# Routed rows outside the 512-row units: 35 units of 128 rows between the large units, in place of 21 units of 256

## The reference, cut to what matters

```
logits = flat @ gate_W.T ; top_v, top_i = top_k(softmax(logits), 2)      # 8 experts, 8192 tokens
g = silu(einsum('td,edf->etf', flat, w1_e)) ; u = einsum('td,edf->etf', flat, w3_e)
out_e = einsum('etf,efd->etd', g * u, w2_e)                              # f = 512
routed = einsum('te,etd->td', gates, out_e)                              # two experts a token
shared = the same form with one expert of width 512 for all tokens, divided by 8
ffn = 0.5 * shared + 0.5 * routed ; out = x + attention(xn) * silu(ffn)
```

## Time and profile before

| what | value |
|---|---|
| median of 3 runs | 722.14 us |
| the profiled execution's span | 719.3 us |
| what lies around its span, against the median | 2.8 us |
| TensorE matmuls busy | 654.1 us, 91% |
| VectorE busy | 555.4 us, 77% |
| ScalarE busy | 494.9 us, 69% |
| GpSimd busy | 478.9 us, 67% |
| mean granted TensorE clock | 0.988 |

### The profile page before, as it was taken

The page is one execution under the profiler, slowest core; times in us unless marked ns, Lnnn a source line. Parts: engine busy times, 40 slices in busy tenths (PEclk is TensorE's granted clock), DMA queues, the critical chain, the costliest instruction groups (busy, mean ns, idle before and its releaser), DMA issues.

```text
span 719.3 us, 22370 instructions
## 1 busy us (share of the span) xinstructions
PE 654.1 (91%) x8536; PEld 452.1 (63%) x8536; DVE 555.4 (77%) x1058; ACT 494.9 (69%) x1008; POOL 478.9 (67%) x519
## 2 busy tenths in 40 slices
PE   2787897978999999999999999999997899999993
PEld 1544565646665665566666666878886676777772
DVE  5989986877667886667766676667664899999996
ACT  4864798857665656666666666666665788888872
POOL 4844321244777777777777777767778487888873
PEclk9999999999999999999999999999999999999997
DMA  9931111111111323433323334333362767777762
GB/s 243 299 95 45 45 61 46 45 51 36 48 49 49 108 91 108 137 108 108 110 92 109 106 106 139 110 101 108 97 103 93 237 179 230 216 229 222 233 176 59
DMA packets 88616, 86.75 MB, mean 121 GB/s; under 512 B 11394, under 2 KB 65284, under 8 KB 88516
## 3 DMA queue, kind: packets, MB, share of 16 engines
q1 hardware_dynamic: 79428, 66.70, 29.8%
q0 software_dynamic: 9088, 18.63, 9.6%
HBM read 50.82 MB, written 34.47 MB: 119 GB/s over the span
## 4 chain that ended last, share of the span: by engine, by line
PE 53%; DVE 13%; ACT 12%; POOL 11%; issue 7%; DMA 3%; SPq 0%; POOLq 0%; DVEq 0%; ACTq 0%
PE banks L1556 7%; PE banks L1558 7%; PE banks L1557 7%; PE banks L1596 5%; DVE hidden L1218 4%; POOL expert_rows L644 4%; PE banks L1576 4%; PE banks L1577 4%; PE banks L1575 4%; POOL srows L634 3%; ACT hidden L785 3%; PE banks L1621 3%; PE banks L1693 3%; PE banks L1672 3%; ACT rows L823 2%
## 5 line engine op out<-in xcount | busy, mean ns | idle before, releaser
L785 ACT CAST hidden<-hidden 128x512 f16<-128x512 f32 x206 | 127.1, 617 | 135.5 <-DVE hidden L1218 135.4
L634 POOL DMA_INDIRECT srows<-normed_rows,source x142 | 149.7, 1054 | 60.4 <-issue 40.2
L1222 DVE TENSOR_TENSOR hidden<-hidden 128x512 f16<-128x512 f32 x180 | 124.4, 691 | 83.9 <-ACT hidden L785 83.0
L1218 DVE TENSOR_TENSOR hidden<-hidden,banks 128x512 f32<-128x512 f32 x206 | 140.8, 684 | 44.0 <-ACT hidden L781 38.2
L1575 PE MATMUL banks<-wwords,hidden 128*128 (+1 forms) x824 | 148.8, 219 | 1.5 <-DVE hidden L1222 1.1
L1576 PE MATMUL banks<-wwords,hidden 128*128 (+1 forms) x824 | 148.6, 219 | 0.0
L1577 PE MATMUL banks<-wwords,hidden 128*128 (+1 forms) x824 | 148.6, 219 | 0.0
L781 ACT ACTIVATE hidden<-banks 128x512 f32<-128x512 f32 x206 | 122.7, 596 | 28.1 <-PE banks L1558 27.8
L1556 PE MATMUL banks<-sx,wwords 128*128 128x512 f16 (+1 forms) x368 | 121.5, 330 | 3.2 <-DVE wwords L1013 2.7
L1558 PE MATMUL banks<-sx,wwords 128*128 128x512 f16 (+1 forms) x368 | 121.6, 330 | 0.0
L1557 PE MATMUL banks<-sx,wwords 128*128 128x512 f16 (+1 forms) x368 | 121.5, 330 | 0.0
(11 more groups left out here) (218 smaller groups left out, 1429.7 us busy)
## 6 DMA issues: line engine op xcount, KB each, us to landing
rows<-x SPq DMA_DIRECT2D x32, 256.0 KB, 4.9
rows<-expert_rows SPq DMA_DIRECT2D x32, 256.0 KB, 3.6
normed_rows<-rows SPq DMA_DIRECT2D x16, 256.0 KB, 3.9
r_rows<-rows SPq DMA_DIRECT2D x16, 256.0 KB, 2.1
rd_rows<-rows SPq DMA_DIRECT2D x16, 256.0 KB, 2.2
stage<-r_rows SPq DMA_DIRECT2D x16, 256.0 KB, 4.0
k_rows<-rows SPq DMA_DIRECT2D x16, 256.0 KB, 2.2
kd_rows<-rows SPq DMA_DIRECT2D x16, 256.0 KB, 2.2
```

The source lines that it names most:

```text
L634: G.indirect_dma_start(srows[:, q % NXB, t, :], None, rows_in, bass.IndirectOffsetOnAxis(source[:, at:at + 1], 0)).then_inc(sem[f"s_in{q % ...
L785: A.copy(guh[:, i % 4, :], gu[:, i % 2, :]).then_inc(sem["gu_hi"], 1)
L1218: V.tensor_tensor(gu[:, i % 2, :], sg[:, i % 2, :], psum[2 * (i % 2) + 1][:, :], ALU.mult).then_inc(sem["gated"], 1)
L1222: V.tensor_tensor(gul[:, i % 4, :], gu[:, i % 2, :], guh[:, i % 4, :], ALU.subtract).then_inc(sem["gu_lo"], 1)
```

## The change

The 21 units of 256 rows become 35 units of 128 rows ("pieces"). A piece has one step that holds all four channel blocks side by side: `columns` gives four blocks of 128 columns, so `pe_up` of a piece is 24 matmuls of 128 columns, with sixteen register instructions, and its `pe_down` twelve matmuls with eight. There are now 16 shared, 25 wide and 35 piece units: 199 steps. Two pieces stand at steps 48 and 49. The other 33 are spread between the 29 large units left, mostly one behind each, so that the pattern is wide, piece, wide, piece.

The groups of a wide unit stay 256 rows (50 of them), that of a piece is 128 rows (35), with buffers of their own (`trows`, `tx`, `ty`, two of each). `flip_step` puts the transposes of a wide unit two and one steps before its first step, and that of a piece one step before, or earlier where the next group would otherwise fall on the same step. GpSimd's order is now by step: `gather_step` is the step behind the transpose that frees the buffer, `scatter_step` a unit's last step plus five. There are 135 gathers and 135 scatters in place of 142 and 142. The `pe_part` steps begin at step 68.

```diff
+        order = [("shared", i) for i in range(FIRST)] + [("piece", i) for i in range(EARLY_PIECES)]
+        large = [("wide", i) for i in range(WIDES)]
+        for m in range(MIXED):
+            large.insert((m + 1) * (WIDES + MIXED) // (MIXED + 1), ("shared", FIRST + m))
+        placed = EARLY_PIECES
+        for n, unit in enumerate(large):
+            order.append(unit)
+            until = EARLY_PIECES + (n + 1) * (PIECES - EARLY_PIECES) // len(large)
+            order += [("piece", i) for i in range(placed, until)]
+            placed = until
...
+        steps = [(v, j) for v in range(NU)
+                 for j in range(1 if order[v][0] == "piece" else 4)]
...
+        for q in reversed(range(GROUPS_IN)):
+            v, h = groups[q]
+            due = first_step_of[v] - (1 if piece(v) else 2 - h)
+            flip_step[q] = min(due, flip_step[q + 1] - 1) if q + 1 < GROUPS_IN else due
+        for q, (v, h) in enumerate(groups):
+            p = last_in_slot(q, NXB, 2)
+            due = FIRST_STEPS - 2 if p is None else flip_step[p] + 1
+            gather_step[q] = max(due, gather_step[q - 1]) if q else due
+            scatter_step[q] = first_step_of[v] + (1 if piece(v) else 4) + LAG + 1
...
-            at = j - (2 if wide(v) else 0) if len(todo) == 1 else j // 2 if wide(v) and j % 2 == 0 else -1 if wide(v) else j
...
-        PART_STEP = 75
+        PART_STEP = 68
...
-            for q in range(ROUTED + SCATTER_LAG):
-                if q < ROUTED:
-                    pool_sorted(q)
-                if q >= SCATTER_LAG:
-                    pool_scatter(q - SCATTER_LAG)
+            for i in range(FIRST_STEPS - 2, NS + LAG + 2):
+                for q in groups_at(i, scatter_step):
+                    pool_scatter(q)
+                for q in groups_at(i, gather_step):
+                    pool_sorted(q)
...
-                return [(2 * j + c, c * UNIT, UNIT) for c in range(2)]
+                return [(c, c * P, P) for c in range(FC)]
...
-                        T.wait_ge(sem["s_lo"], blocks[-1] + 1)
+                        T.wait_ge(sem["s_lo"], mine[-1] + 1)
```

More of the change, by code:

```diff
@@ L34, with constants @@
 CONST = {}
-def constants(routed):
+def constants(ntok):
     p = np.arange(P)
@@ L159, in build @@
         sxh, sxl = [sx[:, i, :, :] for i in range(2)]
+        tx = sb("tx", [P, 2, 2, P], F16)
+        txh, txl = [tx[:, i, :, :] for i in range(2)]
         hidden = sb("hidden", [P, 8 * 2 * UNIT])
@@ L293, in build @@
         FIRST = SHARED - MIXED
[L294 to L308, removed]
+        EARLY_PIECES = 2
+        order = [("shared", i) for i in range(FIRST)] + [("piece", i) for i in range(EARLY_PIECES)]
[8 more added lines that the diff above has]
+            placed = until
         LAG = 3
-        steps = [(v, j) for v in range(NU) for j in range(2 if order[v][0] == "narrow" else 4)]
+        steps = [(v, j) for v in range(NU)
+                 for j in range(1 if order[v][0] == "piece" else 4)]
         NS = len(steps)
@@ L1529, in columns @@
                 v, j = steps[i]
-                if wide(v):
+                if not piece(v):
                     return [(j, 0, WIDE)]
-                return [(2 * j + c, c * UNIT, UNIT) for c in range(2)]
+                return [(c, c * P, P) for c in range(FC)]
             def pe_up(i):
@@ L1539, in pe_up @@
                 if routed(v):
[L1540 removed]
+                    mine = groups_of(v)
                     if v == FIRST and j == 0:
@@ L1543, in pe_up @@
                     if j == 0:
-                        T.wait_ge(sem["s_lo"], blocks[-1] + 1)
-                    q = blocks[0] % RING
-                    mh, ml = [a[:, q:q + len(blocks), :].rearrange("p b i -> p (b i)") for a in (sxh, sxl)]
+                        T.wait_ge(sem["s_lo"], mine[-1] + 1)
+                    mh, ml = pair_of(mine[0])
+                    if not piece(v):
+                        q = ring(mine[0], RING, 2)[0]
+                        mh, ml = [a[:, q:q + 2, :].rearrange("p b i -> p (b i)") for a in (sxh, sxl)]
                 else:
@@ L1738, in pe_program @@
                 if i >= LAG:
-                    load = steps[i][0] + 1 if i < NS and last_step_of(i) and routed(steps[i][0] + 1) else None
+                    load = steps[i][0] + 1 if i + 1 < NS and last_step_of(i) and routed(steps[i][0] + 1) else None
                     pe_down(i - LAG, load)
```

146 lines of the change are left out of this document (89 added, 57 removed).

## The result

The changed kernel takes 766.76 us (median, 763.39 to 767.95), beside 722.94 us for the kernel before on the same chip (four runs; 722.14 was the median of the first three): a ratio of 1.0607 [1.0577, 1.0636]. The forecast was 746.7 with a range up to 765. The sign was right and the size was not. The profiled execution took 766.12 us, with a span of 764.3, 45.0 more than the 719.3 of before.

The account below looks back on a forecast made before the run. TensorE, without gaps, was taken to bound the routed phase: 354.7 work + 29.5 transpose waits + 14.0 feed + 0.4 late gathers = 398.6 us against 374.0, so 722.1 becomes 746.7 us, range 729 to 765.

Parts of the forecast that it names:

- Part 1: Routed phase, TensorE's pure work: fewer steps bring it to 354.7 us, a gain of about 14 us.
- Part 2: Transposes one step before their use: TensorE waits for low halves at wide units and late pieces, 29.5 us (25 to 35).
- The covered ones: Six wide units with an attention part following on TensorE: wait covered but for 0.2 us each, 1.2 in all.
- The late pieces: Six pieces transposed at the step before: one covered by an attention part, five waiting 0.85 us each, 4.3 together.
- Part 3: Feeding TensorE register instructions and an expert's address load for each of 35 pieces: 0.40 us each, 14.0 (0 to 37).
- upper end: Per piece, 0.48 us for the expert's load plus 0.6 for register instructions, about 1.05; 37 us over all pieces.
- the feed-bound one: Sequencer limits every piece: 21 us more, 15 after overlap with waits, about 762 us; chance 0.17.
- Part 4: GpSimd's queue, 14 DMA instructions shorter: no longer behind, late gathers fall from 3.6 to 0.4 us.
- What would show it: Timeline signs: TensorE idle 1.1 to 1.7 us before wide units some 24 times, busy share of the phase about 92%.
- the pair in the list of waits: TensorE's `pe_up` waiting for the low half before wide units: total should go from 0.5 us to over 20.
- "0.07 to 0.09": Spacing in us of a piece's `pe_up` matmuls where the feed limits them, 0.055 otherwise.

Follow-up runs that it names:

- all three at once: Changed kernel with transposes from the fifth group on one step earlier, pieces on expert 0's weights at a fixed address, no expert loads before pieces: 711.87 us, 0.9853.
- the last mended kernel: Changed kernel with transposes a step earlier (pieces' three), experts loaded early, attention parts moved, 26 directly before pieces; everything computed: 715.53 us, 0.9907.

## Why the prediction was right or wrong

**Part 1** held: with the waits and the feed taken away the phase is 361.4, and the costs measured step by step add up to the 62.5 us between 354.7 and 417.2, with nothing left for the pure work to be off by. No other source of gain shows in all three at once and in the last mended kernel, the two that are faster than before.

**Part 2** held as a sum, 29.5 forecast and 29.5 measured, though by luck in its items. Wide units cost 1.04 each, not 1.15 to 1.5: from transpose to `pe_up` 1.85 to 2.00 us, and the lateness behind a part that I took from the earlier trace rows didn't add up, since TensorE waits in between and the others catch up; in the run without loads, where TensorE is sooner, those six units do wait 1.44 to 1.57. The covered ones cost 0.38 each, not 0.2, and for another reason: the part covers the low half in full, and the 0.38 are the gap of the load. So "the load before a wide unit falls into the stall of part 2 and costs nothing" was right at 19 units and wrong at these six, 2.1 us. The late pieces cost 7.4, not 4.3; one of them (step 135) 2.09. The old kernel with late transposes shows the mechanism of the wait by itself at five units, and the run that takes the waits away shows what they hide: the loads before wide units came up, 9.6 us, as soon as their cover was gone.

**Part 3** is the step that failed, in the value that I chose and not in the mechanism. "I take 0.40, nearer the lower end, since the row of the load is of a wholly dry queue" was wrong: 28 of 35 pieces were fed from a dry queue. Measured are 29.3 us, 0.84 a piece, against 14.0; the bounds of 0 to 37 held. In the kernel before, register instructions and loads were hidden, as said: the 461 distances between neighbouring 256-column matmuls of its narrow steps from 171 us on are 0.10 or 0.11, and of 157 `pe_down` only the one of step 51 has a gap at the load, the 0.53 of the earlier trace rows. After, I read the runs so (the trace doesn't show how far the sequencer is): the waits for low halves that stand in front of the transposes and of each wide unit keep it at TensorE's heels, and the 0.67 us of a wide step's `pe_down` are too short to win a lead. Only six pieces directly behind an attention part ran at 1.34, and one two steps behind a part at 1.41. The piece at step 105 stands directly behind a part as well and took 2.21: its own low half was late, and the wait for it stood between the part and the piece. The row of the part was at hand: where long matmuls stand before a piece and no wait between, the feed is free, and where not, the rows of the dry queue are the ones to take. With gaps of the load before 21 pieces, 21 x 0.48 + 28 x 0.6 = 27 would have been the sum. No run shows the 0.6 us of feed in the upper end, with which the 1.05, the 37 and the rival's 21 were made; the runs show 0.66 at each of the 28 pieces, and 0.04 for one register instruction where 0.10 was read from the earlier trace rows. The fixed weights (16.4 us back) and the missing loads (8.8 in the steps before pieces, 6 in the time) confirm both halves.

**The rival** that came true is the feed-bound one, in 28 of the 35 pieces. Its price was 21 over the forecast, 767.7 in full, and I took 6 off for overlap with the waits. There is no overlap, as the feed lies at pieces and the waits at wide units: 766.8 was measured. The range ended at 765, too low by 1.8. That 767.7 lies so near is in part luck: part 3 came to 29.3 and not to 35, and 3.7 came from a cost that nobody had named. By the time of a `pe_up` alone, some 2.0 us, a pace of 0.084 for each pair of weight load and 128-column matmul would have passed as well, and the runs with fixed weights, at 0.055, refute it here.

**Not in the forecast**: 3.7 us of transposes that wait because the one before them, on the step before, has not been copied out. I had looked at who waits for the low half of a group and not at the group behind it. The start of the phase came 2.3 us later, but it lies between 171.0 and 173.4 in the profiles of all these kernels, the old one's variant among them. 2.3 + 43.2 - 0.5 at the end is the 45.0 of the spans.

**Part 4** held: no late gathers, GpSimd waits for results. **What would show it**: TensorE's busy share of the phase is 93% (about 92% said), and the idle before wide units is there 19 times (24 said). But the pair in the list of waits went to 10.8 us and not over 20. At 358.71 the stretch is 1.03 us too long, and only 0.48 of it stand in that line: 0.36 are the load's gap at 357.73, put down to issue or lost in recorded lengths, and 0.165 the recorded length of the last matmul beyond its pace. I had priced by distances and then named a view that counts otherwise. And "0.07 to 0.09" between matmuls of a fed piece was right in the mean (0.25 for three), while each three has two at 0.055 and one at 0.13.

## What to carry to other kernels

Before tiles are made smaller, count what each one needs beside its work (register instructions, loads of an index, waits), and ask of each place whether long work stands directly before it; if the queue is dry there, take the dry queue's price in full (here 0.66 us for the `pe_up` of a piece, and mostly 0.4 to 0.6 for a load). Keep two steps between a producer chain of three engines and its consumer (one step in place of two cost the old kernel 22 us), and check the producer of the group behind it as well. A wait that comes true just before TensorE gets there costs more than its own length: loads and register instructions behind it lose their cover, in the old kernel too (10.4 us of loads behind 9.1 of such waits). A cost that lies inside a wait is not gone: removing the wait alone gave back 20 of 30 us, and only all edits together the whole.

## What the runs showed of the hardware

With a dry queue two register instructions lengthen three 128-column matmuls from 0.165 to 0.25 us, 0.04 each (step 115: 2.01 us with sixteen of them, 1.34 without), in line with one triple after another of the piece at 355.26:
```profile
L1617 PE MATMUL banks<-tx,wwords 128*128 128x128 f16 x280 | 59.0, 226 | 7.4 <-DVE tx L1272 5.9
```
The group's idle time of 7.4 us (part 5 of the page after) holds nothing of it: all of this cost is hidden in matmuls recorded as 0.22 us long. The load of an expert's number into a register leaves mostly 0.4 to 0.6 us between two matmuls of TensorE with a dry queue (0.59 at 353.85, 0.42 at 202.71; 0.10 to 0.67 at 45 places of the kernel after, 41 of them from 0.35 up), and none at step 89 (0.06 from 286.32 to 286.38), whose piece stands behind six 512-column matmuls. With no register instructions in the 24 of a piece's `pe_up`, 36 pairs of weight load and 128-column matmul ran at 0.055 us each (all three at once, from 219.14).
